# A block of gated cross-attention and routed feed-forward: another plan string for TensorE in each of the four kinds of step

## What is computed

```python
# x: (16, 256, 128), ctx_1024: (16, 1601, 128)
qh, kh, vh = heads(layernorm(x) @ wq.T + bq), heads(ctx @ wk.T + bk), heads(ctx @ wv.T + bv)
logits = einsum('bhqd,bhkd->bhqk', qh, kh) / sqrt(8)
out = einsum('bhqk,bhkd->bhqd', softmax(logits), vh)      # softmax over 1601 keys
x = x + tanh(g_xattn) * (merge(out) @ dense_w.T + dense_b)
n = layernorm(x)
scores = sigmoid(n @ gate_W) * route_scale                # best 2 of 8 experts, weights normalised
h = gelu(einsum('bsd,edh->bseh', n, W1) + b1)
y = einsum('bse,bsed->bsd', gate_full, einsum('bseh,ehd->bsed', h, W2) + b2)
x = x + tanh(g_ffn) * (y + gelu(n @ Ws1 + bs1) @ Ws2 + bs2)
```

## Time and profile before

| | us |
|---|---|
| median of 3 runs (lowest to highest) | 1282.12 (1279.38 to 1286.63) |
| the profiled execution's own time | 1285.7 |
| its span, first to last instruction | 1283.6 |
| busy TensorE / VectorE / ScalarE / GpSimd | 1203.1 / 1060.8 / 1050.8 / 350.8 |
| mean granted clock of TensorE, share of full speed | 0.953 |

### The profile page before, as it was taken

One profiled execution on the slowest core, in us unless ns is written; L12 is line 12 of the kernel. 1 busy time (PEld: TensorE's weight loads), 2 busy tenths in 40 slices (PEclk: granted clock), 3 DMA queues, 4 the chain that ended last, 5 costly groups with the idle time before them and its releaser, 6 DMA issues.

```text
span 1283.6 us, 30942 instructions
## 1 busy us (share of the span) xinstructions
PE 1203.1 (94%) x12011; PEld 460.7 (36%) x12011; DVE 1060.8 (83%) x1346; ACT 1050.8 (82%) x1964; POOL 350.8 (27%) x359
## 2 busy tenths in 40 slices
PE   3698999999999999999999999999999999999877
PEld 1223333323334333343334333343334433343234
DVE  5888888879898998989898998889898899989112
ACT  1168879879998999889998899889998899889861
POOL 3461131504242043404233043413324032000100
PEclk7679989989999999999999999999999999999896
DMA  6983526454372545555462655545264655400100
GB/s 168 209 161 86 120 55 143 95 108 113 99 143 71 124 105 122 123 108 121 96 136 66 132 111 108 137 95 120 67 148 86 134 121 105 89 13 26 34 9 9
DMA packets 65587, 132.14 MB, mean 103 GB/s; under 512 B 13721, under 2 KB 40674, under 8 KB 62466
## 3 DMA queue, kind: packets, MB, share of 16 engines
q1 hardware_dynamic: 64510, 129.42, 45.8%
q10 hardware_dynamic: 932, 0.75, 0.2%
HBM read 86.59 MB, written 42.84 MB: 101 GB/s over the span
## 4 chain that ended last, share of the span: by engine, by line
PE 73%; DVE 9%; issue 6%; DMA 5%; ACT 3%; SPq 1%; POOL 1%; ACTq 0%; POOLq 0%; DVEq 0%
PE o_ps L1026 28%; PE a_ps L1008 16%; PE b_ps L990 13%; DVE run_max L1192 6%; PE a_ps L893 5%; PE a_ps L889 3%; DMA vctx<-ctx_t 3%; ACT probs L758 2%; PE a_ps L882 2%; PE b_ps L967 2%; PE b_ps L916 1%; PE a_ps L861 1%; DMA r_dram<-den 1%; ACT L773 1%; PE a_ps L873 1%
## 5 line engine op out<-in xcount | busy, mean ns | idle before, releaser
L758 ACT ACTIVATE probs<-a_ps 128x512 f32<-128x512 f32 (+1 forms) x1664 | 901.9, 595 | 121.2 <-PE a_ps L1008 106.9
L1192 DVE TENSOR_REDUCE run_max<-b_ps 128x2 f32<-128x1024 f32 x767 | 898.1, 1219 | 111.1 <-PE b_ps L990 103.2
L1026 PE MATMUL o_ps<-probs,v_op 128*32 128x256 f32 (+1 forms) x5368 | 507.5, 449 | 1.3 <-ACT probs L758 0.6
L1008 PE MATMUL a_ps<-q_op,k_op 51*128 51x256 bf16 (+1 forms) x3328 | 330.6, 277 | 18.5 <-ACT probs L758 14.6
L990 PE MATMUL b_ps<-k_op,q_op 48*128 48x512 bf16 x2046 | 316.0, 342 | 22.7 <-DVE run_max L1192 16.0
L1008 PEld LDWEIGHTS a_ps<-q_op,k_op 51*128 51x128 bf16 (+1 forms) x3328 | 108.2, 96 | 351.2 <-ACT probs L758 306.4
L1026 PEld LDWEIGHTS o_ps<-probs,v_op 128*32 128x32 f32 x5368 | 107.6, 108 | 188.0 <-issue 114.7
L990 PEld LDWEIGHTS b_ps<-k_op,q_op 48*128 48x128 bf16 x2046 | 87.2, 95 | 141.9 <-DVE run_max L1192 82.4
L653 POOL TENSOR_TENSOR k_parts<-k_t,one 128x400 bf16<-128x400 f32 (+1 forms) x60 | 51.4, 856 | 203.3 <-ACT k_t L779 202.1
L664 POOL TENSOR_TENSOR rstd_q<-rstd_q,minus_half 128x4 f32<-128x4 f32 x8 | 8.7, 1083 | 285.3 <-DVE rstd_q L1092 285.3
L893 PE MATMUL a_ps<-wv_s,vctx 128*128 128x128 f32 (+1 forms) x416 | 66.2, 301 | 5.9 <-DMA vctx<-ctx_t 4.5
(11 more groups left out here) (124 smaller groups left out, 597.8 us busy)
## 6 DMA issues: line engine op xcount, KB each, us to landing
k_op<-k_dram SPq DMA_DIRECT2D x62, 400.2 KB, 6.8
k_dram<-k_parts SPq DMA_DIRECT2D x30, 600.4 KB, 6.4
vctx<-ctx_t SPq DMA_DIRECT2D x16, 800.5 KB, 10.6
k_op<-k_dram SPq DMA_DIRECT2D x62, 200.1 KB, 7.5
kctx<-ctx_t SPq DMA_DIRECT2D x15, 800.5 KB, 4.9
o_dram<-o_s SPq DMA_DIRECT2D x30, 256.0 KB, 2.0
g_all<-g_dram SPq DMA_DIRECT2D x14, 512.0 KB, 6.4
k_dram<-k_parts SPq DMA_DIRECT2D x30, 200.1 KB, 5.8
```

The lines of the kernel that those rows point to most:

```text
L758: act.activation(probs[0:keys, unit % PB, :], a_ps[at % AB][0:keys, :], ACT.Exp, scale=SCALE).then_inc(a_taken, 1)
L1008: last = pe.matmul(a_ps[(at + side) % AB][0:KEYS[t], SEQ * a:SEQ * a + SEQ], k_op[buf][rows, slot, 128 * t:128 * t + KEYS[t]], q_op[buf][r ...
L1026: last = pe.matmul(o_ps[32 * j:32 * j + 32, cols], v_op[s // 2 % 2][0:KEYS[t], t, GP * (s % 2) + j, :], probs[0:KEYS[t], unit % PB, cols], ...
L1192: dve.tensor_reduce(run_max[:, t, :, p, c:c + 1].rearrange("q v o -> q (v o)"), slot[:, :, :], AX.X, ALU.max).then_inc(b_taken, 1)
```

## The change

The four strings of `PLAN` are replaced by four others; nothing else changes. Each string has as many P, S, V, T, k, q, f, y and c as before. The four v of a batch stand in other steps (2, 2, 1 and 3 in the four kinds of step, before 4, 0, 0 and 4), and the d of the third kind has moved to the fourth. Of one string, the first:

```diff
 PLAN = (
-    "PSVPVSPSkVPSVPSVPSVPSkSPVVPSkSPVVPSVPSVPSVPVSPSkSPVVSPSvPSVVPSTVVPSdPvSPVVPSvPSVVSPSVPVv",
...
+    "PSSPVVPSkSPSVVPSkSPVVPSSPVVPSSPVVPSkSPVVPSSPVVSPkSSPVVPSTVVPdPSvPVVPSSPVVPSvSPVVPSVVPS",
...
 )
```

More of the change, by code:

```diff
@@ L85 @@
 PLAN = (
-    "PSVPVSPSkVPSVPSVPSVPSkSPVVPSkSPVVPSVPSVPSVPVSPSkSPVVSPSvPSVVPSTVVPSdPvSPVVPSvPSVVSPSVPVv",
-    "SSPVVPycPSVVSPyPcSPVVPSycSPVVPSVPSVPSVPSVPSVPSVPSVSPVSPycPSTVVPSVPSVPSVPSVPSfVPSVPSfSPSVV",
-    "PVSPVkSPSkPVVPkVPSVPSVPVPSVPSVPSVPSVPSfVPSVPSVPSVPSVPVSPSfffSSTffSPVdSVPSVPSVPSVPSVPSkSPVV",
-    "PSVPVSSPvqSPVVPSVPVSPSvPSVVPSvPSVVPSVPSVPSVPSvVPSSPVVPSVPSVPSVPSTVSPqSPVVPSVPSVPSVPSV",
+    "PSSPVVPSkSPSVVPSkSPVVPSSPVVPSSPVVPSkSPVVPSSPVVSPkSSPVVPSTVVPdPSvPVVPSSPVVPSvSPVVPSVVPS",
+    "yPcSPVVSPSVVPSfSPVVPyPcSPVVSPSVVPSvPSVVSPyPcSPVVSPSvVVPSSPyPSVVPcSPSTVVPSSPVVPSSPVVPSfSPVVS",
+    "PSPVVPSkSPVVPkSPVVPVVPSkPSSPVVPSfSPVVPSfffffSPSVVSvSPVVPSSPSPVVPSSPVVPSkSPSTVVPSSPVVPSSPVV",
+    "SPvSPVVPSvSPSVVPSqSPVVPSSPVVPSSPVVPdSPVVPSSPVVPSvSSPVVPqSPVVPSTVVPSSPSPVVPSSPVVPSSPVV",
 )
```

## The result

The changed kernel takes **1322.2 us** (median of 4 runs, 1318.9 to 1327.8), the one before 1282.1 beside it: a ratio of **1.031**, 95% interval 1.027 to 1.036. It is slower, as forecast, by 40 us where 30 were forecast. The profiled execution took 1322.5 with a span of 1320.4, which is 36.8 more than the span before.

The account below looks back on a forecast made before the run. It held the kernel bound by how long one pair lasts in its surroundings, not one engine's total. Six middle rounds at +3.9 us (150.0 against 146.1), the same for the last, +3 for the first: +30, so 1312; range 1287 to 1344.

Parts of the forecast that it names:

- PW: Interval of a pair with a whole value tile behind it: 1.31 us, 34 of them in a changed round.
- PSS: Interval of a pair with two row units behind it: 1.08 us, the next pair waiting for the ring.
- the wait of 0.5 us for `q_op`: Sign: the first pair of the fourth kind of step waits 0.5 us for `q_op`, once a round.
- the ring: Limit between pairs: a pair waiting only for the exponential of the pair before it starts 1.08 us after it.
- The sum of the prices: Priced intervals of one changed round: 148.8 us for 104 intervals, 149.5 with 0.7 added.
- The 0.7: Added to the new round's sum because the same prices gave 145 for the old strings, measured at 145.7.
- d, priced at 1.18: Interval of a pair with d, priced with y and c at 1.18 us; nine such intervals a round.
- The late T, priced at 0.5: Third kind of step, T four pairs before the end: a new 0.5 us wait once a round, bounds 0 and 2.
- First round: First round, where the start's transfers set much of the pace: taken as +3 us.
- A: Rival: TensorE's own time is the bound, 0.24 us saved on each of 255 value-tile visits; 1221 us, chance 7%.
- C: Rival: row units in twos block TensorE behind VectorE, PSS 1.35, 45 us more; 1357 us, chance 10%.
- D: Rival: more waiting drops the granted clock to 0.50 once a round for about 3 us; 1336 us, chance 6%.

Follow-up runs that it names:

- e7: Changed kernel with d of the first kind of step later and pairs of row units taken apart again in 15 places a round; 1296.5 us (1.012).
- e10: Kernel before with PSVPSV turned into PSSPVV in 18 places of its strings; 1305.0 us (1.022).
- e6b: Changed kernel with work left out: exponentials and full row-unit maxima cover 256 of 512 columns; 1270.6 us (0.993).
- e12: Changed kernel with VectorE's maxima of full row units on 256 of 512 columns, all exponentials kept; 1312.8 us (1.023).
- e1: Changed kernel with d in the first kind of step moved three pairs later, swapped with a row unit; 1311.4 us (1.022).
- e5b: Kernel before with work left out: exponentials and full row-unit maxima cover 256 of 512 columns; 1247.1 us (0.974).
- e8: Changed kernel with exponentials and full row maxima on 256 of 512 columns, and d of the first kind of step later; 1241.9 us (0.972).
- e2: Changed kernel with PSSPVV turned back into PSVPSV in 16 places a round; 1315.3 us (1.025).

## Why the prediction was right, and where it was off

**The mechanism held.** A PW of 1.31 to 1.32, a PSS of 1.08, 0.23 us of idle ScalarE behind most W, half clock in the middle rounds only for 3.4 us, in step 4: all as written. The idle of ScalarE ahead of exponentials went from 121 to 163 us. Nothing on its own list of what would show it wrong (PSS under 1.05, PW under 1.25, rounds at 146) occurred; of its signs only the wait of 0.5 us for `q_op` failed to appear. That the new form costs 0.14 to 0.17 for two intervals is shown by e7 and e10. That the ring is what holds a PSS is shown by e6b and e12, not only argued.

**The round.** Forecast 150.0, measured 150.8. The sum of the prices, 149.5, is what e1 shows without d's wait (149.5), but that it fits so well is partly luck. The 0.7 in it stands for what steps 16 to 19 of the kernel before took over their prices, and that was the wait for `vctx` (step 16 takes 37.21 with it, step 8 36.40 without), which the new plan does not have. Without the 0.7 the sum is 148.8, and what makes up for it is a number of intervals a little dearer than priced: those with one k, v, q or f take 31.8 together for 31.0, those with T 6.8 for 6.4. The same holds for the difference of the plans: in steps without waits or half clock a round takes 149.8 in e1 and 144.9 before, 4.9 more, and the waits and half clock of the old plan give 1.3 of that back in its mean of 146.1. The difference between 150.0 and 150.8 comes from two terms:

- *d, priced at 1.18.* "A pair with a y, c or d 1.18" took the d of the first kind of step for one that waits for nothing. It took 1.91 in step 16 and up to 3.45 in step 8, with what follows it about 1.3 a round. The forecast says that "SyncE's other DMAs stand where they stood", and by the table above the divide ends within 3 us of where it did; but d was moved forward by two pairs, and what it waits for was not. The forecast worked out such a lead for T, but not for d, which before had 2.1 us to spare at most. This is the mis-sized term that matters: 11 us.
- *The late T, priced at 0.5.* In step 18 SyncE's issues began at 785.81, 5.09 us before the pair that needs them, more than the 4.7 put down; the last one ended 1.08 before it, less than the 1.4 put down, and still the pair did not wait. TensorE waited 1.0 us for `nm_t` in the whole kernel, 0.7 before. The term should have been zero, its lower bound.

Smaller ones: a v with a row unit on both sides 1.86 for 1.63, the hidden units 9.10 for 9.0, W with S 1.54 as priced.

**The ends.** First round +0.1 for +3. Why it did not grow stays open. That the start's transfers set the pace there is not shown: with ScalarE's and VectorE's work shortened, the first round of e5b takes 143.9 in place of 152.8. Last round +8.7 for +3.9: in step 28 d waited 2.06 us, which was followed by 3.4 us at half clock, 3.6 together over before; e1 takes 3.3 of these back. The second to fourth steps add 2.1, 2.1 and 0.9.

**The rivals.** *A* did not happen. TensorE's busy time did fall by 14 us, so fewer visits cost it less, but this was freed inside intervals which the ring holds open. Its price of 0.24 a visit was also too high: in e8, with the ring at 0.87, two intervals in the new form take 2.19 against 2.22 in the old. The Trainium skill's rules (TensorEngine Tiling (Array Packing), Key Properties, on the drain at a change of tiling mode; Perfetto Trace Analysis, Matmuls, on larger matmuls) name costs that many small visits pay more often. The trace agrees with them on TensorE's own time, by 0.03 in two intervals, and not on a gain for the kernel. *C* showed once a round, as a PSS of 1.38, and e12 prices VectorE at about 9 us in all, not 45. *D* came to the middle rounds once, behind d's wait in step 4; there the clock is 1.00, a little better than before (0.99). In e2 it came in nearly every round, behind longer waits of d.

**What stays open.** e7, with d in time and the pairs apart, is still 15 us behind the kernel before by its span: 1.3 in each of the six middle rounds, 3.6 in the first and 3.9 in the last. In steps without waits or half clock it is 2.6 a round: the second and third kinds of step are 1.7 and 1.6 longer than before, the first 0.45 and the fourth 0.24 shorter. Its whole tiles that stand alone behind a pair, and the v's moved to the second and third kinds of step, lie in that rest; no run took them apart.

## What to carry to other kernels

Where engines are balanced, a plan is priced by the interval from one pacing unit to the next, with each engine's and each buffer ring's limit beside it; work gathered into larger pieces makes long and short intervals, and the short ones do not fall below the ring's. A unit that is moved forward needs the time at which its own data arrive, along the whole chain of its transfers, also when these have not been touched. And a change that makes everything ahead of such a wait faster gains little until the wait is moved too: in the profiled executions e2 alone gained 0.15 us a middle round, with e1 beneath it nearly the same edit gained 2.05 (by the medians 7 us and 15).

## What the runs showed of the hardware

*A small transfer behind a large one.* In step 16 of the changed kernel 16 KB were issued 1.9 us behind 800 KB on SyncE's queue. The small one landed 9.0 us after its issue and the large one 10.7 after its own, so within 0.2 us of each other. In step 18, where the same 800 KB had gone out 7.6 us ahead, the 16 KB landed after 3.7 us. No run moved the small transfer ahead of the large one.

*The clock behind a single wait.* In step 28 of the changed kernel d stood 2.06 us, and the granted clock of the next 3.4 us was 0.50 (1.2 GHz): a v took 1.97 us in place of 1.16 and a whole tile 1.60 in place of 1.06. The length of the wait alone does not tell whether the clock falls. In step 4 a wait of 1.52 was followed by 3.4 us at 0.51, in step 8 one of 2.44 was not, and the v behind it took 1.16 (windows and TensorE's timeline of the changed kernel):

```profile
1149.00:1152.50 3.50, 1.44 (x13) 0.92 (x12) 1.03 (x3) 1.39 (x3) 0.72 (x1) 1.00 0.09 26
1152.50:1155.90 3.40, 3.40 (x20) 1.82 (x19) 2.51 (x11) 2.37 (x5) 1.79 (x2) 0.50 0.00 1
399.00:402.40 3.40, 3.22 (x30) 1.98 (x30) 2.31 (x12) 1.95 (x4) 3.16 (x5) 1.00 0.04 9
...
399.18 0.68 PE L916 MATMUL b_ps<-wd_s,attn 128*128 128x128 f32 x4 [2.44 <-POOL attn L693]
...
400.34 1.16 PE L893 MATMUL a_ps<-wv_s,vctx 128*128 128x128 f32 x8
...
1151.16 0.68 PE L916 MATMUL b_ps<-wd_s,attn 128*128 128x128 f32 x4 [2.06 <-POOL attn L693]
...
1152.31 1.97 PE L893 MATMUL a_ps<-wv_s,vctx 128*128 128x128 f32 x8
...
1154.75 1.60 PE L1026 MATMUL o_ps<-probs,v_op 128*32 128x512 f32 x8
```
